# A seventh shared piece ahead of the sixth, shared weights loaded inside the tile loop, and another order of the small engines' work around the tiles

## What is computed

```python
x = x + 0.5 * ffn(_layernorm(x), ...)
x = x + attn(_layernorm(x), ...)
x = x + 0.5 * ffn(_layernorm(x), ...)
```

```python
shared_out = jax.nn.silu(g_s) * u_s @ shared_w_down.T
logits = x2 @ gate_w.T
probs = jax.nn.softmax(logits, axis=-1)
topk_vals, topk_idx = jax.lax.top_k(probs, TOP_K)
...
gu = jnp.einsum('th,eih->eti', x2, w_gate_up)
g, u = jnp.split(gu, 2, axis=-1)
act = jax.nn.silu(g) * u
out_e = jnp.einsum('eti,ehi->eth', act, w_down)
moe_out = jnp.einsum('eth,te->th', out_e, combine)
return (moe_out + shared_out).reshape(orig_shape)
```

## Time and profile before

| | |
|---|---|
| time, median of three runs | 1164.51 us (1162.78 to 1164.62) |
| time of the profiled execution | 1161.62 us |
| its span | 1159.9 us |
| PE matmul busy | 1110.0 us (96%) |
| DVE, ACT, POOL busy | 670.8, 571.6, 465.4 us |
| granted TensorE clock, mean | 0.988 of full speed |
| DMA, mean over the span | 99 GB/s |

### The profile page before, as it was taken

The page is one execution under the profiler, slowest core; times in us unless marked ns, Lnnn a source line. Parts: engine busy times, 40 slices in busy tenths (PEclk is TensorE's granted clock), DMA queues, the critical chain, the costliest instruction groups (busy, mean ns, idle before and its releaser), DMA issues.

```text
span 1159.9 us, 19606 instructions
## 1 busy us (share of the span) xinstructions
PE 1110.0 (96%) x6008; PEld 930.1 (80%) x6008; DVE 670.8 (58%) x1810; ACT 571.6 (49%) x1514; POOL 465.4 (40%) x484
## 2 busy tenths in 40 slices
PE   8889998799999999999999999999999998899996
PEld 6667876588888888888888888888888876678875
DVE  7568867744545444545454445454454547668866
ACT  4257752555546445545444454544553533257750
POOL 1546647125315315324423432522532320546644
PEclk9989999999999999999999999999999999999998
DMA  9985565001101101000110010010000006935556
GB/s 357 414 325 190 186 225 185 16 1 37 56 1 37 55 0 36 22 32 0 36 54 0 36 54 0 36 54 0 36 0 1 1 1 269 372 112 176 189 157 197
DMA packets 38617, 114.80 MB, mean 99 GB/s; under 512 B 4384, under 2 KB 4384, under 8 KB 36512
## 3 DMA queue, kind: packets, MB, share of 16 engines
q1 hardware_dynamic: 33440, 97.30, 23.1%
q0 software_dynamic: 5120, 16.78, 4.2%
HBM read 79.20 MB, written 34.87 MB: 98 GB/s over the span
## 4 chain that ended last, share of the span: by engine, by line
PE 89%; DVE 4%; issue 3%; ACT 2%; DMA 1%; DVEq 0%; SPq 0%; ACTq 0%
PE bank L1363 23%; PE bank L1432 15%; PE bank L1448 9%; PE bank L1398 9%; PE bank L1338 7%; PE bank L1252 6%; PE bank L1376 6%; PE bank L1349 4%; PE bank L1271 3%; PE bank L1299 2%; PE bank L1444 1%; PE bank L1394 1%; DMA xn<-x_rows 1%; PE bank L1231 1%; PE bank L1188 1%
## 5 line engine op out<-in xcount | busy, mean ns | idle before, releaser
L538 POOL TENSOR_TENSOR scores<-scores,pinv 128x512 f32<-128x512 f32 (+3 forms) x256 | 176.7, 723 | 360.6 <-DVE pinv L1081 360.6
L481 POOL TENSOR_TENSOR tback_lo<-experts,tback_hi 128x768 fp32r<-128x768 f32 x62 | 114.3, 1845 | 82.4 <-ACT tback_hi L644 82.4
L744 ACT ACTIVATE oT_hi<-bank 128x512 fp32r<-128x512 f32 x64 | 38.3, 598 | 208.7 <-PE bank L1444 208.7
L732 ACT ACTIVATE scores<-scores,nmax 128x512 f32<-128x512 f32 (+3 forms) x256 | 140.3, 558 | 0.6 <-DVE nmax L1071 0.5
L706 ACT ACTIVATE pT_hi<-bank 128x512 fp32r<-128x512 f32 (+2 forms) x192 | 86.8, 487 | 108.0 <-PE bank L1376 108.0
L1051 DVE TENSOR_TENSOR pT_lo<-bank,pT_hi 128x512 fp32r<-128x512 f32 (+2 forms) x192 | 100.9, 553 | 48.3 <-ACT pT_hi L706 48.3
L1071 DVE CUSTOM_DVE_ANT_0 scores<-bank,causal 128x512 f32<-128x512 f32 (+3 forms) x256 | 112.2, 486 | 1.5 <-issue 0.5
L1363 PE MATMUL bank<-xnT_hi,wqs_hi 128*128 128x512 f32 x256 | 106.4, 416 | 0.9 <-DVE x L962 0.9
L1432 PE MATMUL bank<-wds_hi,oT_hi 128*128 128x512 f32 x256 | 105.9, 414 | 1.4 <-DVE oT_lo L1055 1.4
L1055 DVE TENSOR_TENSOR oT_lo<-bank,oT_hi 128x512 fp32r<-128x512 f32 x64 | 44.3, 691 | 108.6 <-ACT oT_hi L744 108.6
L1363 PE MATMUL bank<-xnT_lo,wqs_hi 128*128 128x512 f32 x256 | 100.8, 394 | 0.0
(11 more groups left out here) (206 smaller groups left out, 2885.2 us busy)
## 6 DMA issues: line engine op xcount, KB each, us to landing
experts<-in_ffn_w SPq DMA_DIRECT2D x32, 768.0 KB
xn<-x_rows SPq DMA_DIRECT2D x62, 256.0 KB, 2.7
y_rows<-xn SPq DMA_DIRECT2D x62, 256.0 KB, 2.1
raw_q<-in_wq SPq DMA_DIRECT2D x8, 1024.0 KB
raw_d<-in_wd SPq DMA_DIRECT2D x8, 1024.0 KB
x_rows<-experts SPq DMA_DIRECT2D x1, 7936.0 KB, 29.7
raw_w<-in_ffn_w SPq DMA_DIRECT2D x8, 768.0 KB, 5.6
raw_kv<-in_wkv SPq DMA_DIRECT2D x8, 512.0 KB, 3.3
```

The lines of the kernel that those rows point to most:

```text
L481: nc.gpsimd.tensor_tensor(tback[par][1][:], experts[:, bass.ds(at + FRONT, GU - FRONT)], tback[par][0][:].bitcast(F32), ALU.subtract).then ...
L538: nc.gpsimd.tensor_tensor(s, s, pinv[k % 2][:, i:i + 1].to_broadcast([P, P * (i + 1)]), ALU.mult).then_inc(att.normed, 1)
L732: nc.scalar.activation(s, s, ACT.Exp, bias=nmax[par][:, i:i + 1], scale=-1.0, accum_out=psumr[par][:, i:i + 1]).then_inc(att.exp, 1)
```

## The change

It keeps every matmul and changes where things stand.

- Router: the second half's logits go to bank 4 instead of 3, so that three matmuls of piece 1 can stand ahead of the fold; `rank` follows one chunk later.
- First tiles: the high half of tile 1's `back` is cut ahead of the loop (ScalarE, GpSimd), the cut of the third `wdn` moves from ahead of the loop into step 1, and the additions of piece 3 are split, two ahead of the loop and two in step 0.
- Loads: tile 6's load stands ahead of the last two experts' loads, and the load of the last shared pair moves from the end of the tiles to just ahead of tile 8's load. It gets places of its own, `wgu_late` and `wdn_late`.
- Last tile: `gate_up` of piece 5, gate half, is cut in two around the last `turn_hidden`, and the last pair's gate/up weights are cut as soon as the last tile's matmuls are done.
- After the tiles: piece 6 comes ahead of 5. TensorE's order is gate_up 6, down 4, the up half of 5, down 6, gate_up 7, down 5, and down 7 in two halves, in the first part with attention's turn between them.
- VectorE makes the first low halves of attention (`first_lows`), and ScalarE makes all six high halves ahead of the high half of piece 6. GpSimd issues its 16 gathers in one go.
- At the very end `combine` and `add_down` alternate.

```diff
@@ feed_forward, SyncE @@
-                for e in left[3:]:
+                for e in left[3:5]:
                     load_expert(e)
-                for k in range(4):
+                load_tile(n, 1, 2)
+                for e in left[5:]:
+                    load_expert(e)
+                store_tile(n, 0, 0)
+                load_tile(n, 1, 3)
+                for k in range(1, 4):
                     store_tile(n, 0, k)
-                    if k < 2:
-                        load_tile(n, 1, k + 2)
+                load_shared(n, 3)
...
@@ routed, ScalarE @@
+                    if j == 1:
+                        cut_dn(n, BEFORE // 2)
-                    if j <= TILES - 2:
+                    if 0 < j <= TILES - 2:
                         back(1 - par, at[k + 2], there[k + 2] if n == 0 and j < EARLY_TILES else 2 * LOADED_HALF)
...
+                    if j == TILES - 1:
+                        cut_gu(n, NSH - 1)
...
                 front(at[1])
+                act.wait_ge(ffn[n].act_lo, BEFORE)
+                act.wait_ge(ffn[n].d_mm, HALF * (BEFORE - 1))
+                back(1, at[2], there[2] if n == 0 else 2 * LOADED_HALF)
                 turned(0, 1)
-                cut_dn(n, BEFORE // 2)
...
@@ feed_forward, ScalarE @@
-                shared(n, BEFORE + 1, SLOTS - 2)
+                gate(n, BEFORE + 1)
+                gate(n, SLOTS - 2)
+                cut_dn(n, NSH - 1)
                 if n == 0:
                     act.wait_ge(loaded.kv, 16)
                     first_cuts(high_part, 0, 2)
-                shared(n, SLOTS - 2, SLOTS - 1)
-                if n == 0:
                     act.wait_ge(loaded.q, 16)
                     first_cuts(high_part, 2)
+                high(n, SLOTS - 2)
+                high(n, BEFORE + 1)
...
@@ VectorE @@
+                    if j == 0:
+                        add_down(n, BEFORE - 1, range(HALF // 2, HALF))
+                    if j == TILES:
+                        low_gu(n, NSH - 1)
...
-                add_down(n, BEFORE - 1)
+                add_down(n, BEFORE - 1, range(HALF // 2))
...
+            def first_lows(first, last):
+                def low_part(hi, lo, raw, count):
+                    dve.wait_ge(att.w_hi, count)
+                    nc.vector.tensor_tensor(lo, raw, hi.bitcast(F32), ALU.subtract).then_inc(att.w_lo, 1)
+
+                first_cuts(low_part, first, last)
...
@@ TensorE @@
                     if isinstance(j, int) and j == TILES:
+                        gate_up(n, BEFORE + 1, (0,), range(0, HC // 2))
                         turn_hidden(j, par)
+                        gate_up(n, BEFORE + 1, (0,), range(HC // 2, HC))
...
-                gate_up(n, BEFORE + 1)
+                gate_up(n, SLOTS - 2)
                 pe.wait_ge(moe[n].y_out, TILES)
                 down(n, BEFORE)
-                gate_up(n, SLOTS - 2)
-                gate_up(n, SLOTS - 1, (0,))
+                gate_up(n, BEFORE + 1, (1,))
                 down(n, SLOTS - 2)
-                gate_up(n, SLOTS - 1, (1,))
+                gate_up(n, SLOTS - 1)
                 down(n, BEFORE + 1)
+                down(n, SLOTS - 1, range(0, HALF // 2))
                 if n == 0:
                     turn_norm(1, 0)
-                down(n, SLOTS - 1)
+                down(n, SLOTS - 1, range(HALF // 2, HALF))
```

More of the change, by code:

```diff
@@ L495, in routed @@
                 back(0, at[1], 1)
+                back(1, at[2], 2)
                 low_dn(n, BEFORE // 2)
@@ L1170, in _ @@
             feed_forward(1)
[L1171 removed]
             low(1, SLOTS - 1)
             combine(1, 4)
+            add_down(1, SLOTS - 1, range(HALF // 2))
             combine(1, 6)
[L1175 removed]
+            add_down(1, SLOTS - 1, range(HALF // 2, HALF))
         @block.tensor
@@ L1240, in gate_up @@
                 pe.wait_ge(norm[2 * n].lo, HALF * (tb + 1))
-                wait(pe, f.mul, s - 1)
+                if s >= 2:
+                    pe.wait_ge(f.mul, DOWN_AT[s - 2] + 1)
+                if s == 1:
+                    pe.wait_ge(route[n].out, 1)
+                w = gate_weights(s // 2)
                 for half in halves:
```

131 lines of the change are left out of this document (74 added, 57 removed).

## The result

The changed kernel took 1182.96 us (median of four runs, 1179.25 to 1184.37) where the kernel before took 1163.8 us beside it. The ratio is 1.0147, with a 95% interval of 1.0124 to 1.0171. The medians are 19 us apart, and the two profiled executions 21 us (their last work ends at 1178.25 and 1157.18 us). The forecast was 1160.0.

A forecast was written before the change was run, and what follows sets the result against it. TensorE, busy 1110.0 of 1159.9 us, was taken as the bound. Terms 0 - 2.0 - 0.95 + 1.2 + 0 - 2.8 summed to -4.5 us, against a median of 1164.5 giving 1160.0, range 1154 to 1166.

The forecast's parts named there:

- Slower: Rival: stops in gathers or scatters move; one of 7.9 us bare on TensorE's path gives +3.4, 1168 us; chance 0.14.
- The stops: Waits for "remote" beside scatters and gathers: 7.23 us in the first part, 7.89 and 3.77 in the second, cause unnamed.
- 12.0 us of VectorE's work: End of the second part: VectorE's chain from TensorE's last gate/up at 1142.4 to 1154.4, where before ended at 1157.2.
- the -2.8: End of the second part: gain from VectorE ending at 1154.4 instead of 1157.2; bounds -4 and 0.
- Router: Three matmuls ahead of the fold fill its 0.65 us wait, swallowed by the scatter's stop: 0; bounds 0 and -1.3.
- First tiles: Tile 2 of each part starts about 1 us earlier: -1.0 a part, -2.0 in all; bounds -3.9 and -1.0.
- Loads in the loop: Tile loop: tile 6's 0.95 us wait goes; tile 8 waits 0.6 us a part, +1.2 together, bounds 0 and +3.8.
- End of the first part: Before attention: queries' weights land at 173.2, VectorE's chain ends at 189.4 against 189.07; net 0, bounds -1.5 and +3.
- later than 175: End of the first part: sign of being wrong, if the queries' weights, expected at 173.2, land after 175 us.
- the same: Rival: both tile loops stall 1.9 us on tile 8, tile 7 waits; -1.0 in all, 1163.5 us; chance 0.18.

The follow-up runs named there:

- e5: The changed kernel as it is, run again on a second chip: 1153.42 us, ratio 0.9996 to the kernel before.
- e6: The kernel before as it is, run again for a profile on the second chip: 1147.89 us in one run.
- e8: The kernel before with the router's part of the change alone: 1152.91 us, ratio 1.0009 to the kernel before.
- e12: The changed kernel with attention's six first low halves made on GpSimd after its eighth gather of part 1, none on VectorE: 1158.49 us, ratio 1.0059.
- e2: The changed kernel with GpSimd waiting after its eighth of 16 gathers until piece 7 is multiplied, both parts: 1160.06 us, ratio 1.007.
- e10: The changed kernel with the gathers in two runs of eight in both parts, as e2, on a third chip: 1158.47 us, ratio 1.0056.
- e4: The changed kernel with GpSimd waiting after its eighth of 16 scatters until piece 3's up half is made, both parts: 1164.68 us, ratio 1.0104.

## Why the prediction was wrong

The forecast of 1160.0 fell on the wrong side, and the rival "Slower" came true, to which I had given 0.14 and a price of 7.9 us. The profiled executions, cut at the same points (first gate/up matmul of tile 0, last gate/up matmul of the tiles, first projection, the statistics of part 2's second half), show where. The last two columns are the changed kernel minus before, in us, on the chip of the first pair and on the second chip (e5 minus e6):

```
stretch                              forecast   first pair   undisturbed
start to tile 0, part 1                 0           +4.5        +2.3
tiles, part 1                          -1.4         +1.7        +0.9
last tile to attention                  0           +7.0        +3.5
attention                               0           -0.6        +1.2
to tile 0, part 2                       0           +4.2        +1.2
tiles, part 2                          -0.4         +0.2        -0.1
last tile to the end                   -2.8         +4.2        -2.8
sum                                    -4.5        +21.1        +6.2
```

The undisturbed column is of single executions, and e6 was a quick one (4.3 us under its kernel's median; its clock was lowered in two stretches only, e5's in four). By the medians the sum there is +1.2. The first pair costs 14.9 us more than the undisturbed one, and the four stretches beside indirect DMAs alone make 15.5 of it.

*The stops.* The step that failed is "They were 7.23 us in the first part, 7.89 and 3.77 in the second ... each in a stretch of gathers or scatters ... no row shows what the stops wait for". I took them as given lengths that might land on another instruction, and in the sum that gives 1160.0 their change has no term: it is 0. They are increments of TensorE held back while a run of GpSimd's transfers lasts, so their length is set by how far into the run an increment falls, and the change moved piece 7 deeper into one. In part 1 the kernel before was also helped by GpSimd's pause after twelve gathers: piece 7's gate was held there too, but only until 186.48. The diff removes the pause, and I did not cost that. At the kernel's end 12.0 us of VectorE's work behind the last gate/up were right (11.6 from 1166.62 to 1178.25), but it started 7 us late, and the -2.8 became +4.2. The Trainium skill, "Runtime: NRT & Kernel Launch", section "Instruction fetch mechanics", on which I leaned for this rival, is not what makes the stops: the trace records when blocks of program are fetched, and in the changed kernel none is fetched between 181.4 and 200.5 us, nor between 46.7 and 72.0, where stops are. One is fetched in the last stop, at 1154.2, and so it is in e5, at 1132.5, where nothing stops.

*Router.* "the stop behind the scatter swallows what TensorE is ahead" was wrong in its first half. TensorE is not ahead: the three matmuls ahead of the fold wait for the same copy as the fold did, since `gate_up` now waits for `route[n].out`. The fold comes 1.2 us later (26.55 for 25.39 us), TensorE ran 3.4 us at half clock behind it, and the scatter starts at 37.79 in place of 35.31. Undisturbed it starts 1.0 us later and takes 1.2 more. e8 puts the part's price at 1 us, interval -1.4 to +3.5; the forecast was 0 to -1.3.

*First tiles.* Right in kind, a little too good in size. From tile 0 to tile 2 the changed kernel needs 6.05 us where before needed 6.88, in both parts, and undisturbed in part 2: -0.83 for my -1.0. It is also the 0.8 which followed from the Trainium skill, "SBUF — State Buffer", section "Who interferes with whom". The first pair's trace agrees: tile 2's tfront_lo ends at 82.14, just behind the first of GpSimd's two tback_lo (two in 3.80 us from 80.04). Undisturbed in part 1 it is only -0.3 (6.59).

*Loads in the loop.* Tile 6's 0.95 us are gone. Tile 8 waits, as forecast, but for 2.4 us in part 1 and 0.7 in part 2 of the first pair (2.2 and 1.2 undisturbed), where I had 0.6 each and a bound of 1.9. The weights landed in 7.7 us, not in 5.6. Gains and losses of the tiles cancel.

*End of the first part.* I had the queries' weights landing at 173.2 and named "later than 175" as a sign of error. They landed at 180.5, 6.5 us from an issue that came 7.3 us later than before (173.95 for 166.64). VectorE's statistics came at 203.0 for my 189.4. Undisturbed, they come 29.7 us after the last gate/up matmul of the tiles, before 25.9: the 4.1 us of low halves are that difference in size, and my net 0 lacked them, since I had set them against waits of VectorE that are filled with other work. But e12 shows that taking them off VectorE gains nothing, so what remains shown is the size at this place, not that the low halves could be had for less.

*Chances.* On undisturbed chips this change is "the same", my 0.18. That the chip of before was in a condition that others are not, nothing I read in its trace told; the holes in its record of landings, had I counted them, could have been a hint. Its stops for "remote" could have told that part of this kernel's time hung on something unnamed; on other chips it takes 10 to 13 us less.

## What to carry to other kernels

Before you price a stop for "remote" or "issue", look in the trace's semaphore records for when the increment arrived and which instruction made it; if the maker had long ended, the wait's length belongs to what runs beside it and will change with the order. Work that others wait for should not be put deep into a run of GpSimd's indirect DMAs: cut such a run with a wait that TensorE's chain releases, where what it delays has room. On the chips without late increments such a cut wins nothing, and where the end of the kernel hangs on the gathers it costs: e2 and e10, cut in both parts, are 0.6 to 0.7% slower than the kernel before. When a result surprises, run both kernels again on another chip before explaining it by the order of instructions.

## What was unexpected in the hardware

- In the first pair and on one of six chips (before 1163.8 and 1165.57 us) TensorE's increments of semaphores arrive up to 10.0 us late while GpSimd's indirect DMAs run; on five chips, none is over 1 us late. The DMA packets themselves took as long in either condition (129 and 129 ns in the first scatter, 184 and 184 ns in the last gathers of the kernel before), so bandwidth is not the likely cause. ScalarE's cut of a product of VectorE starts at once in these stretches (1151.67 us for a multiply that ends at 1151.64). A run of eight, then a pause, left none of piece 7 late, and three of piece 6 up to 2.7 us late. What the condition is stays open, and so is the part of the recording, which is full of holes in just these three traces. Whether a shorter run would always be enough wasn't tried. The scatter in two (e4) never met the condition, so what it would be worth there is open too.
- Weighted additions on VectorE with two inputs in SBUF took 10.27 us for four beside GpSimd's subtractions, and 2.73 us without (e12, e5): here VectorE bears the whole loss, and GpSimd's 128x512 subtraction takes 1.3 us as in the kernel before.
- The issue of an indirect DMA took 1.76 us beside a VectorE subtraction with two inputs in SBUF, and 1.04 us without.
